# Spreading GpSimd's sorted-row scatters over the dense part of a two-layer macaron block

## The reference

```python
scores = jax.nn.softmax(xt @ router_w, axis=-1)
expert_weights, expert_idx = jax.lax.top_k(scores, TOP_K)
h = gelu(jnp.einsum('td,edf->tef', xt, w1)) * jnp.einsum('td,edf->tef', xt, v1)
y = jnp.einsum('tef,efd->ted', h, w2)
yk = jnp.take_along_axis(y, expert_idx[:, :, None], axis=1)
out = jnp.sum(expert_weights[:, :, None] * yk, axis=1) + bias
```

## Time and profile before

| | |
|---|---|
| timed runs (3), median | 482.81 us |
| timed runs, lowest and highest | 482.15 and 485.86 us |
| profiled execution: span, first to last instruction | 502.7 us |
| mean granted TensorE clock in the profiled execution | 0.966 |
| TensorE matmul busy in it | 441.0 us (88%) |
| VectorE, ScalarE, GpSimd busy in it | 311.2, 248.2, 237.4 us |

### The profile page before, as it was taken

How to read it: one execution, slowest core, us unless ns; L and a number is a source line. 1 busy time by engine, 2 the same in 40 slices (tenths; PEclk the granted TensorE clock), 3 DMA queues, 4 the chain that set the end, 5 groups by cost and what they waited for, 6 DMA issues and landing times.

```text
span 502.7 us, 10906 instructions
## 1 busy us (share of the span) xinstructions
PE 441.0 (88%) x3447; PEld 369.0 (73%) x3447; DVE 311.2 (62%) x935; ACT 248.2 (49%) x585; POOL 237.4 (47%) x321
## 2 busy tenths in 40 slices
PE   1998859899999898699999999999779969999990
PEld 1877648788899775577777777777459958888880
DVE  3765645976867485295959586756526744544672
ACT  4744434436444456255556565555465524554541
POOL 7365658556453413044454545432525467534441
PEclk9999959999999999899999999999999989999997
DMA  8971111122331010230212120200112223122522
GB/s 236 290 116 38 48 58 33 50 75 75 91 85 54 30 48 15 71 85 17 60 50 61 47 63 30 64 24 3 70 37 61 64 60 96 53 65 72 171 80 78
DMA packets 50633, 35.51 MB, mean 71 GB/s; under 512 B 5754, under 2 KB 47706, under 8 KB 50538
## 3 DMA queue, kind: packets, MB, share of 16 engines
q1 hardware_dynamic: 45140, 23.90, 18.9%
q0 software_dynamic: 4784, 10.54, 6.3%
q10 hardware_dynamic: 656, 0.40, 0.3%
HBM read 15.37 MB, written 13.01 MB: 56 GB/s over the span
## 4 chain that ended last, share of the span: by engine, by line
PE 65%; DVE 9%; issue 8%; ACT 5%; POOL 4%; DMA 3%; another core or an unknown queue 2%; ACTq 1%; SPq 1%; POOLq 0%; DVEq 0%
PE bank L1490 9%; PE bank L1483 6%; PE bank L1587 5%; PE bank L1472 5%; PE bank L1473 4%; PE bank L1474 4%; PE bank L1626 4%; PE bank L1611 4%; PE bank L1444 3%; PE bank L1590 2%; PE bank L1591 2%; PE bank L1462 2%; PE bank L1614 2%; PE bank L1434 2%
## 5 line engine op out<-in xcount | busy, mean ns | idle before, releaser
L538 POOL DMA_INDIRECT yp<-scr,dest x77 | 76.5, 994 | 90.8 <-ACT scr L770 71.1
L877 ACT ACTIVATE stage<-bank 128x512 f32<-128x512 f32 x128 | 74.6, 597 | 72.6 <-PE bank L1615 63.7
L1263 DVE TENSOR_REDUCE nm<-bank 128x2 f32<-128x512 f32 x128 | 84.0, 685 | 38.4 <-PE bank L1591 35.8
L1490 PE MATMUL bank<-wd,scr 128*128 (+1 forms) x462 | 64.9, 277 | 1.3 <-ACT scr L763 1.3
L1472 PE MATMUL bank<-wu,xbT 128*128 x154 | 63.1, 410 | 2.1 <-DVE xbT L1129 1.8
L1137 DVE COPY scr<-bank 128x256 f32<-128x256 f32 x77 | 32.5, 422 | 51.5 <-PE bank L1483 22.8
L1490 PEld LDWEIGHTS bank<-wd,scr 128*128 128x128 f32 (+1 forms) x462 | 60.7, 193 | 1.8 <-issue 1.7
L1587 PE MATMUL bank<-qk_rows 126*128 126x256 bf16 x256 | 50.8, 280 | 4.9 <-DMA qk_rows<-lev 4.2
L1611 PE MATMUL bank<-qk_rows 128*128 128x256 bf16 x256 | 50.3, 279 | 3.7 <-DMA qk_rows<-wd 3.0
L1473 PE MATMUL bank<-wu,xbT 128*128 x154 | 50.8, 330 | 0.0
L1474 PE MATMUL bank<-wu,xbT 128*128 x154 | 50.8, 330 | 0.0
(11 more groups left out here) (218 smaller groups left out, 949.3 us busy)
## 6 DMA issues: line engine op xcount, KB each, us to landing
qk_rows<-lev SPq DMA_DIRECT2D x96, 64.0 KB
scr<-xs SPq DMA_DIRECT2D x77, 64.5 KB
stage<-yp SPq DMA_DIRECT2D x8, 256.0 KB, 3.2
scr<-yp SPq DMA_DIRECT2D x6, 256.0 KB, 3.1
stage<-in_w SPq DMA_DIRECT2D x8, 176.0 KB, 3.4
stage<-in_v SPq DMA_DIRECT2D x8, 176.0 KB, 4.3
xs<-qk_rows SPq DMA_DIRECT2D x3, 451.5 KB
yp<-scr,dest POOLq DMA_INDIRECT x77
```

The source lines that it names most:

```text
L538: nc.gpsimd.indirect_dma_start(out=yp[PHASE[n]][:, :], out_offset=bass.IndirectOffsetOnAxis(ap=dest[:, n:n + 1], axis=0), in_=ysb[:, n % Y ...
L877: nc.scalar.activation(probs[:, g % RING, kt, 2 * (hp % 2):2 * (hp % 2) + 2, :], psS2[(b * 16 + j) % 3][:, :].rearrange("p (h n) -> p h n" ...
L1263: nc.vector.tensor_reduce(nm[:, qt, 2 * hp:2 * hp + 2], psS1[i % 2][:, :].rearrange("p (h n) -> p h n", h=2), AX.X, ALU.max, negate=True). ...
L1490: i = nc.tensor.matmul(ph[n % len(ph)][:, 3 * P:4 * P], hTs[0:w, n % 2, k * P:(k + 1) * P], wd[0:w, bass.ds(experts[n], 1), k, :].rearrang ...
```

## The change

GpSimd's 24 scatters of sorted rows are issued in six groups of four. Each group but the first waits for a product of the dense part: for `down_done` 6, 9, 12, 15 and 18. The bias of a chunk is added behind its second group. The two transfers of zeros come last, behind `down_done` 21. The transfers, their sizes and what they write are the same, and so are the waits of all other engines.

```diff
             pool.wait_ge(numbered, 3)
-            for c in range(1, 4):
-                scatter(0, c, lambda t, k: xn1[:, t - DT, k, :], scat1)
+            for c, first, second in ((1, 0, 6), (2, 9, 12), (3, 15, 18)):
+                for half, down in enumerate((first, second)):
+                    if down:
+                        pool.wait_ge(down_done, down)
+                    at = 4 * c + 2 * half
+                    scatter(0, c, lambda t, k: xn1[:, t - DT, k, :], scat1, range(at, at + 2))
+                add_ffn_bias(0, c)
+            pool.wait_ge(down_done, 21)
             zero_scatter(0)
-            for q in range(1, 4):
-                add_ffn_bias(0, q)
 
             pool.wait_ge(scat1, 16 * 2 * (NT - DT))
             pool.wait_ge(zero_landed[0], 32)
```

## The result

The change takes 492.33 us, the median of four runs (487.52 to 493.74), against 484.34 us for the kernel before (482.15 to 486.98, four runs): ratio 1.0145, 95% interval 1.0098 to 1.0191. 492.0 was forecast. The profiled execution of the change took 492.05 us and spans 490.2 us; that of before spanned 502.7.

What follows compares the result with a forecast made beforehand. TensorE's stops beside long scatter runs were taken to bound the profiled execution, hardly the timed runs. Timed: 482.8 + 0 (groups) + 6.7 (late zeros) + 2.6 (clock) = 492.1, say 492; range 477.5 to 495.5.

Steps and rivals of the forecast that it cites:

- its first step: Whole kernel: TensorE's stops beside long scatter runs belong to the profiled execution's recording; timed runs hardly have them.
- The size of the stops: Profiled execution before: idle TensorE and half clock in the dense part and two later places cost 24.8 us together.
- The dense part's term: Dense part, 35.4 to 76.4 us: 9.2 us idle and 3.9 lost at half clock, 13.1 us of stops.
- The two later places: Near 360 and 404 us, six transfers in a row each: stops and low clock cost 4.1 and 7.6 us.
- The coincidence: Profiled span without stops, 502.7 - 24.8 = 477.9, nearly meets the timed median, 4.9 us above; hence timed runs hardly have stops.
- Part 1: Scatters in six groups, dense part: profiled execution gains 13.1 us, timed runs 0; bounds 0 to -13.1, nothing positive.
- Part 2: Joint of dense and block part: zeros issued last delay the first transposes by 6.7 us; bounds 6.0 to 7.7.
- Part 3: Behind the joint's gap: TensorE's clock falls to half, costing 1.9 + 0.7 = 2.6 us; bounds 0 to 3.9.
- The hidden rest: Behind the joint: late clearings, layer norm scalars and SyncE's wait stay hidden by the delay, adding nothing.
- The first: Rival: timed runs have the stops as the trace does, so all parts count: 479.0 us; chance 0.28.
- The second: Rival: the joint costs only its waits, the clock doesn't fall: 489.5 us; chance 0.08.
- The third: Rival: stops are real, follow the scatters' share of time and stay; only the joint counts: 492 us; chance 0.06.

Runs made afterwards that it cites:

- e7: Kernel before with each chunk's bias between its two halves of scatters, no waits added, on a chip without stops: 484.75 us, ratio 1.0008.
- e10: The change, unchanged, on the third chip, one with stops: 501.38 us, ratio 0.9932 against the kernel before.
- e1: The kernel before, unchanged, run again on a chip with stops: 506.49 us, ratio 1.003.
- e2: Kernel before with only the zeros held back behind product 20, scatters as before, on a chip with stops: 514.51 us, ratio 1.0186.
- e8: The kernel before, unchanged, on the third chip, one with stops: 506.58 us, ratio 0.9988.
- e9: Kernel before with each chunk's bias between its two halves of scatters, as in e7, on a chip with stops: 500.84 us, ratio 0.9904.
- e11: The change without the zeros' wait for product 20, the kernel of e3, on the third chip, with stops: 500.95 us, ratio 0.9891.
- e12: The change with later groups behind earlier products, zeros before the last bias without wait, products 22 and 23 before the transposes; chip with stops: 499.2 us, ratio 0.9808.
- e3: The change without the zeros' wait for product 20, on a chip with stops: 498.65 us, ratio 0.9881.
- e4: The change with 56 unread transposes on TensorE ahead of the block part, on a chip with stops: 500.64 us, ratio 0.9896.
- e5: The change, unchanged, on a chip without stops: 493.18 us against 484.07 for the kernel before, ratio 1.0195.
- e6: The change with products 22 and 23 ahead of the table wait and first transposes, chip without stops: 489.33 us, ratio 1.0108 against before.

## Why the prediction was right, and where it wasn't

**The stops (its first step).** What was assumed of these timed runs holds: TensorE doesn't stop in them. Shown: the old order on a chip without stops has TensorE busy 46.00 of 46.00 us (e7), and the change spans 490.2, 3.0 above 502.7 - 24.8 + 9.3 = 487.2. The reason given doesn't hold as it was put. It was to be recording against no recording, and "no timed run has them". But on three chips timed runs of the kernel before take 505 to 509 us. It is the chip, or its state at the time, that differs. The prediction took the profile and the times for two views of one thing, and on the trace of a chip with stops it forecast 498.9 for the changed profile: that is near e10's span of 497.5, and the profile of the change, from the other kind, has 490.2.

The records still mark the two kinds. The traces should hold 384 recorded landings for the 24 scatters of sorted rows (16 for each). Counted from the traces:

```
chips with stops:    before 94, e1 109, e2 100, e8 100, e9 132, e10 200, e11 176, e12 182, e3 181, e4 177
chip without stops:  the change 384, e5 384, e6 384, e7 384
```

On chips with stops, half to three quarters of these landings are missing. Ranked by the kernel, those with long runs keep 94 to 132 and those with groups of four 176 to 200.

The Trainium skill has it that the notification block's internal pipeline holds producers back rather than lose a record, and that the block counts such stalls; and, as another thing, that in one of its settings records are discarded when a queue's ring is full (NOTIFIC — the notification-queue block, section "Overflow: three behaviours, one of which stalls the engine"). The counts don't speak against that rule: stops and missing records come on the same chips. But they don't come in the same stretches. e3, e10 and e11 miss half of these landings while TensorE doesn't stop in the dense part. Nor could the counts prove the rule, as no run here was without records. Whether such a chip stops when nothing is recorded stays open.

**The size of the stops: 24.8 us was too much.** From the trace of before to e7's the spans fall by 502.7 - 482.4 = 20.3. The dense part's term was right: the first block moves from 89.93 to 76.51, 13.4 us, for 13.1 forecast. The two later places were put at 11.7, and only 20.3 - 13.4 = 6.9 came off. The coincidence by which the prediction chose its side was weaker than it looked: what lies around a span is 1.9 us, so 482.8 - 1.9 = 480.9 stood against 477.9.

**Part 1, the groups: "nothing positive" is the step that failed.** Groups alone leave the gap at 6.08 and 6.28 us (e3, e11). The bound rested on who waits behind GpSimd, and missed that GpSimd's own program has the zeros behind the sixth group: that group can't begin before product 17 (at 65.30 in the change), and 4 transfers, a bias and the first zeros' transfer put the second at 73.45 (the change) or 73.75 (e11), with the wait for product 20 or without it. Its other half, that GpSimd keeps up with pauses of 0.6 to 2 us, holds: 0.5 to 2.5. So do the 13.1 us that it takes off where there are stops: product 20 starts 13.8 us sooner in e10 (70.61) than in e8 (84.37), and 12.6 sooner when each is counted from its first scatter (28.29 and 29.50).

**Part 2, the zeros: right in size, wrong in its landmark.** From the end of product 20 to the transposes 8.8 us were forecast, and the trace has 80.70 - 71.88 = 8.8. Term by term: 0.1 to GpSimd was 0.3; 1.26 to the second issue was 1.29; 3.4 to its landing was 3.35; 4.0 for table, loads and landing was 3.9. The gap itself, against the old order without stops: from the start of product 21 to the transposes 7.58 us (73.12 to 80.70) against 1.36 in e7, +6.2 where +6.7 was forecast, 0.3 of the difference being e7's own wait for its loads.

What the prediction didn't see is how thin the cover was. It had the rows "long loaded" before. In e7 the zeros are issued at 65.04 and the loads are 0.31 late: three biases, 3.9 us, ahead of them and a landing 2.2 us longer than in the change use up all the slack. Without them (issue at 61.1, and 7.3 us from there) the loads of the old order are ready some 6 us before the transposes are due, an estimate from these rows. In the change, e2, e11 and e12 the transposes start 7.2 to 7.4 us behind the second zeros' issue (73.45 to 80.70, 82.67 to 90.08, 73.75 to 81.11, 71.15 to 78.55); in e7 it is 9.4, with the longer landing of the last section. So without a gap the zeros had to be issued by some 67 us (74.14, when the transposes were due in e7, less 7.3), and the change has them at 73.45, 6.6 us behind that.

**Part 3, the clock: 2.6 was 1.9 at the first block, and less may be left of it later.** From the start of the transposes to the first block it takes 3.94 us (80.70 to 84.64) against 2.06 in e7 (74.45 to 76.51): +1.9, as forecast for products and transposes. The 0.7 behind them isn't there: from the first block to the landmark at L1487 (L1483 in e7), where TensorE waits 2.07 us for ScalarE, 25.19 us in the change and 25.27 in e7. So whatever the blocks lost at 1.2 GHz was regained by the time of that wait. e4 shows that the clock stays up when TensorE has work in the gap, and also that only 0.6 to 0.9 us of the 1.9 are left at that wait. So of the 8 us at that wait some 1 is neither the gap nor undone by keeping the clock up, and where it arises stays open.

**The hidden rest** holds for the change. GpSimd sets its first layer norm scalars at 88.30, forecast for 88.4, and waits for nobody, and the landmark at L1487 is later by 8.05 us, no more than the first block. With the clock kept up (e4) it may not hold, as said above.

**The sum.** +6.2 and +1.9 make 8.1 at the first block (84.64 - 76.51), 8.05 at the landmark, 7.8 in the spans (490.2 - 482.4) and 8.0 in the medians. 9.3 was forecast from 482.8, which had been the median of three runs; with the fourth it is 484.34. So 492.0 against 492.33 is nearer than its terms, and that is luck: the term was 1.3 too large, and the median of before 1.5 too low. The side itself was chosen by a coincidence of two sums and given a reason that the runs don't bear out.

**The rivals.** The first (stops in the timed runs as in the trace) is right on the other kind of chip: its sum has -3.8 us, and e10 came out at -5.3 against the median beside it, ratio 0.9932. The second, joint without clock, is out as to its condition: the clock is 0.50 in the third stretch of the profile after. How much of its price is right isn't shown: by e4 the low clock accounts for 0.6 to 0.9 us at L1487. The third has the stops stay in groups of four, and that is out: from 28.3 to 72.9 us TensorE is idle for 0.1 us in e3, e10 and e11, and for 9.2 in before. But that the stops come with scatters per time isn't out. The share of time that the transfers take, at 1.26 us each from the first to the last, is 0.85 in before, 0.83 in e2, 0.79 in e9, 0.77 in e12 and 0.72 in the change, and TensorE's idle time in that window falls in nearly the same order: 9.2, 6.6, 6.7, 0.6 and 0.1 us. No run holds that share fixed and alters the runs.

## What to carry to other kernels

When a profiled execution stands several per cent above the timed runs, find out first whether both come from the same kind of chip: run the old kernel again with a profile beside its times, and look whether untouched places differ between two traces. When transfers are spread, work out the latest time at which the last of them may be issued (here some 7.3 us ahead of its reader) and count everything that the issuing engine has between the release and it, other small work too. Work that doesn't need the late data belongs in front of the wait for it in the reading engine's program (e6: 1.85 us at the place, 3.9 in the time).

## What the runs showed of the hardware that was not expected

There were two kinds of chips, or of states of them: one kernel, unchanged, takes 505 to 509 us on three of them and 484 on a fourth, with TensorE stopping for up to 5.6 us beside runs of GpSimd's scatters on the first kind, and busy 46.00 of 46.00 us beside the same runs on the second. One edit (e7, e9) is worth nothing on one kind and 1% on the other (1.0008 and 0.9904), and the change itself has opposite signs (1.0195 and 0.9932).

The clock can fall after a short wait: in e12 TensorE waited 1.32 us once, with 0.48 us of work in 1.80 us, and the granted clock was 0.53 for the 3.1 us from 80.60.

The zeros' transfer of 128 times 4,128 bytes took 3.35 us from issue to landing in the change, where a bias and 0.52 us of pause stood between it, with the small one, and the scatters. In e7, straight behind four scatters, it took 5.55 us (the chain of waits of e7):

```profile
65.04 5.55 DMA xs<-qk_rows,zpos
```

The scatters ahead of it are not the reason. In e12 both transfers of zeros stand straight behind four scatters, and the clearings, which wait for their landing, begin 3.45 us behind the second (71.15 to 74.60), just as in the change (73.45 to 76.90); in e7 it is 5.66. In before it stands behind eight scatters and landed 3.4 us behind its issue. Two things differ in e7. The instruction took 1.46 us, where 0.96 is usual. And of its packets in the DMA record all but the last four had begun by 68.34; at 68.15 a packet of 16,384 bytes of the queue for instructions took 0.92 us, and the last four, the last of them at 69.93, began from 69.06 on, when it was through. In e12 and in the change no such packet falls between the issue and the landing. So it looks like one load of instructions in the way of a DMA engine; it was seen once and not tested.
